# Four edits to a vision tower on one core: order of clearing, maxima and weight loads; routing constants placed once; the wait for sent rows moved

## The reference

```
h = tok(x)                                   # linear projection of patches
h = LN(h + mlstm(h));      h = LN(h + bit_ffn(h))
h = LN(h + performer(h));  h = LN(h + attention_and_moe_gelu(h))   # 8 experts, top 2
h = LN(h + spectral(h));   h = LN(h + moe_swiglu(h))               # 16 experts, top 2, + 2 shared experts
h = LN(h + quantised_attention(h)); h = LN(h + moe_relu(h))        # 8 experts, top 1
```

## Time and profile before

| what | value |
| --- | --- |
| runs of the kernel | 2841.95, 2848.2, 2851.45 us; median 2848.2 |
| profiled execution: own time | 2844.44 us |
| its span, first to last instruction | 2842.6 us |
| busy PE / DVE / ACT / POOL | 2283.0 / 1468.1 / 895.3 / 893.9 us |
| mean granted PE clock | 0.853 of full |
| moved by transfers | 225.44 MB, mean 79 GB/s |
| stages, from about: route gelu, blocks | 956, 1034 us |
| spectral, route swiglu, shared | 1250, 1662, 1713 us |
| blocks swiglu, quantised, route relu, blocks | 1966, 2325, 2620, 2667 us |

### The profile page before, as it was taken

The page is one execution under the profiler, slowest core; times in us unless marked ns, Lnnn a source line. Parts: engine busy times, 40 slices in busy tenths (PEclk is TensorE's granted clock), DMA queues, the critical chain, the costliest instruction groups (busy, mean ns, idle before and its releaser), DMA issues. The chain is left out here.

```text
span 2842.6 us, 47911 instructions
## 1 busy us (share of the span) xinstructions
PE 2283.0 (80%) x18049; PEld 2006.4 (71%) x18049; DVE 1468.1 (52%) x3564; ACT 895.3 (31%) x1923; POOL 893.9 (31%) x809
## 2 busy tenths in 40 slices
PE   7999975599699759956888967998999977553793
PEld 7888863477588649954666667998999966532692
DVE  2667766456577632237888852222442236846313
ACT  0333326423154213324454411111111113754112
POOL 0332325600110342245665406000111136443424
PEclk9989975599799769977999968999999988555696
DMA  9500000060000435530000006001666631000453
GB/s 258 169 1 1 1 1 18 12 201 2 1 2 2 142 103 173 176 95 15 10 10 5 1 2 244 1 1 75 214 213 213 208 124 41 1 1 2 168 176 90
DMA packets 127066, 225.44 MB, mean 79 GB/s; under 512 B 17201, under 2 KB 97645, under 8 KB 119798
## 3 DMA queue, kind: packets, MB, share of 16 engines
q1 hardware_dynamic: 116278, 204.09, 21.9%
q0 software_dynamic: 10560, 18.29, 2.2%
...
## 5 line engine op out<-in xcount | busy, mean ns | idle before, releaser
L2513 POOL COPY bl_swiglu_w<-ahead_w2swiglu_w 128x1152 f32 x53 | 60.7, 1148 | 478.0 <-PE psum L2557 275.4
L2539 PE MATMUL psum<-bl_swiglu_xt,bl_swiglu_w 128*128 128x128 f32 x1272 | 153.0, 277 | 4.6 <-DMA bl_swiglu_w<-in_swiglu_w 3.6
L2539 PEld LDWEIGHTS psum<-bl_swiglu_xt,bl_swiglu_w 128*128 128x128 f32 x1272 | 151.0, 194 | 5.2 <-DMA bl_swiglu_w<-in_swiglu_w 4.0
L2581 ACT ACTIVATE bl_swiglu_sg<-psum 128x384 f32<-128x384 f32 x106 | 52.0, 490 | 310.5 <-PE psum L2546 310.5
L2608 DVE COPY bl_swiglu_xt<-psum 128x256 f32<-128x256 f32 x53 | 22.5, 424 | 206.5 <-PE psum L2524 206.5
L2692 PE MATMUL psum<-tower_xT,shared_w 128*128 128x216 f32 x528 | 103.1, 353 | 18.9 <-DMA shared_w<-in_shared_w 18.9
L2593 ACT ACTIVATE bl_gelu_hid<-psum,bl_gelu_w 128x128 f32<-128x128 f32 x270 | 74.5, 375 | 124.4 <-PE psum L2546 124.4
L2692 PEld LDWEIGHTS psum<-tower_xT,shared_w 128*128 128x128 f32 x528 | 98.5, 195 | 19.7 <-DMA shared_w<-in_shared_w 19.1
L2557 PE MATMUL psum<-bl_swiglu_w,bl_swiglu_hid 128*128 128x192 f32 x636 | 112.1, 326 | 0.0
L2737 DVE TENSOR_TENSOR shared_hid<-shared_sg,psum 128x432 f32<-128x432 f32 x66 | 39.9, 604 | 134.1 <-ACT shared_sg L2728 128.6
L2513 POOL COPY bl_gelu_w<-ahead_w2gelu_w 128x1350 f32 x45 | 58.9, 1312 | 152.5 <-DVE bl_gelu_y L2628 137.2
...
## 6 DMA issues: line engine op xcount, KB each, us to landing
...
```

What stands on the lines that cost most here:

```text
L2513: pool.tensor_copy(w2[:, n % DEEP], w2all[:, e, :].rearrange("p e n -> p (e n)")).then_inc(s_w2, 1)
L2539: pe.matmul(up_tile(n, j, i, side), w[:, o:o + 128], xt[:, n % 2, side, :], start=(i == 0), stop=False, skip_group_check=True)
L2581: act.activation(sg[:, j], bank_pair(n, j)[:, 0, 0:3 * BLOCK].rearrange("p (i n) -> p i n", i=3), ACT.Silu).then_inc(s_silu, 1)
```

## The change

1. A new ahead plan's transfers go before older ones in `coming`.
2. The routing constants (14 transfers: eight constants, two parts of each of three gate weights) get SBUF for the whole run and are loaded once, by SP in the performer stage before it clears the shelves. The routings wait on the one semaphore `laid`. The seed column is copied by DVE into `base`. The table `blocks` becomes a row `count` that is broadcast. Each routing has two semaphores less, the blocks one less and no gb transfer.
3. The shared experts' weights become an ahead plan. `load_ahead` now also runs in swiglu's route, with the four shared weights, swiglu's second weights (9216 KB) and the quantised stage's; the shared stage's PE waits on one semaphore that SP raises when all of these have landed.
4. POOL no longer waits for its sent rows in the routings; SP waits for them in the blocks stage, between the first block's weights and its rows. For the first three blocks weights are issued ahead of rows; later blocks keep rows ahead of weights. POOL's own wait in the shared stage stays.
5. Spectral: only the edges of hs that must be zero and its row of ones are cleared, ahead of power(0); fetch(1), fetch(2) and the clearing of zz come after it; power(2) moves ahead of the wait for theta and angles(0).
6. Quantised: POOL's clearing of sel and q3 moves behind its power and fetch loop; the maxima of q, k and v are taken one pair later than that of h; the casts into sel move into the score loop.

The diff, cut to its core:

```diff
@@ -137,7 +137,7 @@
         for key, plan in self.plans:
             self.key = key
             self.cst["ahead"][key], dmas = plan(self, self.A)
-            self.cst["coming"] += dmas
+            self.cst["coming"] = dmas + self.cst["coming"]
         return self
...
@@ -1387,6 +1387,7 @@
             def _(sp):
                 S.arrived(sp, s_w)
                 S.clear_before(sp)
+                lay_constants(sp, cst)
                 clear_rows(sp, cst, 1)

...
+def routing_constants(S, cst, A):
+
+    new = {"iota": ([T, 16], A["iota"][:, 0]), "earlier": ([T, T], A["before"]), "ones": ([T, T], A["ones"][0:T, 0:T]),
+           "seed": ([T, 16], A["seed"]), "count": ([1, MAXB], A["blocks"]), "upto": ([16, 3, 16], A["upto"]),
+           "steps": ([16, 1], A["steps"]), "gb": ([128, 4], A["gelu_gb"])}
+    cst["laid"], cst["lay"] = S.sem("laid"), []
+    for name, (shape, src) in new.items():
+        cst[name] = S.sb(name, shape)
+        cst["lay"].append((cst[name][:], src))
+    for kind, E in EXPERTS.items():
+        w = cst["wg" + kind] = S.sb("wg" + kind, [128, 2, E])
+        cst["lay"] += [(w[:, 0], A[kind + "_gate"][0:128]), (w[64:128, 1], A[kind + "_gate"][128:D])]
+
+
+def lay_constants(sp, cst):
+
+    for dst, src in cst["lay"]:
+        sp.dma_start(dst, src).then_inc(cst["laid"], 16)
+
...
 def make_route(kind):
...
-            wg = S.sb("wg", [128, 2, E])
-            iota = S.sb("iota", [T, 16])
-            before = S.sb("before", [T, T])
-            ones = S.sb("ones", [T, T])
-            blocks = S.sb("blocks", [1, MAXB, E])
-            upto = S.sb("upto", [16, 3, 16])
-            steps = S.sb("steps", [16, 1])
-            gb = S.sb("gb", [128, 4])
+            wg, iota, before, ones, count, upto, steps, gb = [
+                cst[k] for k in ("wg" + kind, "iota", "earlier", "ones", "count", "upto", "steps", "gb")]
+            laid, all_laid = cst["laid"], 16 * len(cst["lay"])
...
-            (s_w, s_late, s_z, p_T, c_T, p_l, c_lo, c_m, p_m, c_slot, v, c_all, p_n, c_nb, p_e, c_d, c_e) = S.sems(
-                *"w late z p_T c_T p_l c_lo c_m p_m c_slot v c_all p_n c_nb p_e c_d c_e".split())
-            early = [(wg[:, 0], A[kind + "_gate"][0:128]), (wg[64:128, 1], A[kind + "_gate"][128:D]),
-                     (iota[:], A["iota"][:, 0]), (base[:, 0], A["seed"][:, 0:E]), (before[:], A["before"]),
-                     (ones[:], A["ones"][0:T, 0:T])] + ([(gb[:], A["gelu_gb"])] if gelu else [])
-            late = [(blocks[:], A["blocks"][:, :, 0:E]), (upto[:], A["upto"]), (steps[:], A["steps"])]
+            (s_z, p_T, c_T, p_l, c_lo, c_m, p_m, c_slot, v, c_all, p_n, c_nb, p_e, c_d, c_e) = S.sems(
+                *"z p_T c_T p_l c_lo c_m p_m c_slot v c_all p_n c_nb p_e c_d c_e".split())

...
-                    for dst, src in early:
-                        sp.dma_start(dst, src).then_inc(s_w, 16)
-                    for dst, src in late:
-                        sp.dma_start(dst, src).then_inc(s_late, 16)
                     S.clear_before(sp)
-                    if kind != "swiglu":
-                        S.load_ahead(sp)
+                    S.load_ahead(sp)
...
                 def _(pool):
...
-                        pool.wait_ge(cst["sent"], cst["sent_count"])
...
-                    pe.wait_ge(s_w, 16 * len(early))
+                    pe.wait_ge(laid, all_laid)
                     done = 0
...
                     if gelu:
                         for p in range(3):
                             level(p)
-                    dve.wait_ge(s_w, 16 * len(early))
+                    dve.wait_ge(laid, all_laid)
+                    K.then(dve.tensor_copy(base[:, 0], cst["seed"][:, 0:E]))
...
@@ -2260,7 +2268,7 @@
                         dve.tensor_tensor(lo[:, :, 0:E], lo[:, :, 0:E], highest, ALU.subtract).then_inc(c_d, 1)
                     dve.wait_ge(p_e, 1)
                     upper = lambda j: bank(UP)[:, j * E:(j + 1) * E]
-                    K.then(dve.tensor_tensor(past[:, 0], blocks[:, 0:NB], upper(1)[0:1].unsqueeze(1).broadcast_to([1, NB, E]), ALU.is_ge))
+                    K.then(dve.tensor_tensor(past[:, 0], count[:, 0:NB].unsqueeze(2).broadcast_to([1, NB, E]), upper(1)[0:1].unsqueeze(1).broadcast_to([1, NB, E]), ALU.is_ge))
...
@@ -2452,14 +2460,14 @@
             hid = S.sb("hid", [128, 2, KC, BLOCK])
             sg = S.sb("sg", [128, 2, 3, BLOCK])
             y = S.sb("y", [128, 2, D])
-            gb = S.sb("gb", [128, 4])
+            gb = cst["gb"]
...
             with nc.Block() as block:
                 @block.sync
                 def _(sp):
-                    def fetch_block(n):
+                    def fetch_rows(n):
                         if n >= DEEP:
                             sp.wait_ge(p_T, n - DEEP + 1)
                         b = bass.ds(sp.value_load(place[0:1, n:n + 1], min_val=0, max_val=E * DEPTH - 1), 1)
                         sp.dma_start(xr[:, n % DEEP], shelves[b].rearrange("b p n -> (b p) n")).then_inc(s_x[n % DEEP], 16)
+
+                    def fetch_weights(n):
                         e = bass.ds(sp.value_load(owner[0:1, n:n + 1], min_val=0, max_val=E - 1), 1)
                         if n >= DEEP:
...
                     S.clear_before(sp)
-                    if kind == "gelu":
-                        sp.dma_start(gb[:], A["gelu_gb"]).then_inc(s_gb, 16)
                     for n in range(DEEP):
-                        fetch_block(n)
+                        fetch_weights(n)
+                        if n == 0:
+                            sp.wait_ge(cst["sent"], cst["sent_count"])
+                        fetch_rows(n)
                     S.arrived(sp, s_all)
                     for n in range(NB):
                         if n + DEEP < NB:
-                            fetch_block(n + DEEP)
+                            fetch_rows(n + DEEP)
+                            fetch_weights(n + DEEP)
...
+
+def weights_shared(S, A):
+
+    w1 = [S.sb(f"w1{x}", [128, 3 * 768]) for x in range(SHARED)]
+    w2 = [S.sb(f"w2{x}", [128, 6, D]) for x in range(SHARED)]
+    return (w1, w2), [pair for x in range(SHARED) for pair in (
+        (w1[x][:], A["shared_w1"][x]), (w2[x][:].rearrange("p k n -> p (k n)"), A["shared_w2"][x]))]
...
-        w1 = [S.sb(f"w1{x}", [128, 3 * HID]) for x in range(N)]
-        w2 = [S.sb(f"w2{x}", [128, KC, D]) for x in range(N)]
+        w1, w2 = cst["ahead"]["shared"]
         hid = S.sb("hid", [128, 2, KC, C])
         sg = S.sb("sg", [128, 3, 2, C])
...
-        s_up, s_silu, s_hid, s_dn, s_acc = S.sems("up", "silu", "hid", "dn", "acc")
+        s_w, s_up, s_silu, s_hid, s_dn, s_acc = S.sems("w", "up", "silu", "hid", "dn", "acc")
...
         with nc.Block() as block:
             @block.sync
             def _(sp):
+                S.arrived(sp, s_w)
                 S.clear_before(sp)
-                for x in range(N):
-                    sp.dma_start(w1[x][:], A["shared_w1"][x]).then_inc(s_w[x], 16)
-                    sp.dma_start(w2[x][:].rearrange("p k n -> p (k n)"), A["shared_w2"][x]).then_inc(s_w[x], 16)
-                S.load_ahead(sp)
...
-                    pe.wait_ge(s_w[x], 32)
+                    pe.wait_ge(s_w, 1)
...
                             pe.wait_ge(s_hid, (n - 1) * 3 + j + 1)
@@ -2899,18 +2915,22 @@
                         C_.fetch(pool, 2 * p + 1)

                 fetch(0)
+                for b in range(2):
+                    hi = hs[0:CH, b].rearrange("p s k (g n) -> p s k g n", n=IMG)
+                    for s in range(1, 4):
+                        ins = pool.memset(hi[:, s, :, :, 0:s], 0.0)
+                F_.then(ins)
+                F_.then(pool.memset(hs[CH:CH + 1, :, 0, 1, :], 1.0))
+                C_.power(pool, 0)
                 fetch(1)
-                F_.then(pool.memset(hs[0:CH], 0.0))
-                F_.then(pool.memset(hs[CH:CH + 1], 1.0))
-                C_.power(pool, 0)
-                fetch(2)
                 F_.then(pool.memset(zz[:], 0.0))
                 shifts(0)
+                fetch(2)
                 C_.power(pool, 1)
                 fetch(3)
+                C_.power(pool, 2)
                 pool.wait_ge(s_theta, 1)
                 angles(0)
-                C_.power(pool, 2)
                 fetch(4)
                 scales(0)
                 shifts(1)
@@ -3394,13 +3414,13 @@
                 pool.memset(rnd[:, 1:2], -ROUND).then_inc(s_fix, 1)
                 for t in range(WAY):
                     C_.fetch(pool, t)
-                pool.memset(sel[:], 0.0).then_inc(s_fix, 1)
-                pool.memset(q3[:], 0.0).then_inc(s_fix, 1)
                 for p in range(NP):
                     C_.power(pool, p)
                     if p + 2 < NP:
                         C_.fetch(pool, 2 * p + 4)
                         C_.fetch(pool, 2 * p + 5)
+                pool.memset(q3[:], 0.0).then_inc(s_fix, 1)
+                pool.memset(sel[:], 0.0).then_inc(s_fix, 1)
...
@@ -3732,6 +3752,8 @@
```

(21 more changed lines are left out.)

18 lines of the change are left out of this document (8 added, 10 removed).

## The result

The changed kernel takes 2808.17 us (median of four runs, 2806.78 to 2818.38) where the kernel before takes 2848.53 (2841.95 to 2851.45): ratio 0.9869, 95% interval 0.984 to 0.9898, 37 us by the ratio and 40 by the medians.

What follows compares the result with a forecast made beforehand. Stages bounded by their last engine at each barrier, with standing at the edges. Terms −4.8 − 7.3 − 2.4 − 8.9 + 0.3 − 7.2 − 4.0 = −34.3 us, from the 2848.2 median 2813.9, given as 2814; range 2803 to 2828.

Steps and rivals of the forecast that it cites:

- first stage: First stage, where transfers set the end: the new order of ahead loads was to stay within ±1 us.
- shared: Shared stage: with weights loaded ahead, TensorE starts 0.2 after the barrier; −8.9 us, bounds −9.2 and 0.
- quantised: Quantised stage: clears moved from the start, maxima out of the loop's circle, casts costing some; −7.2 us (0 to −10).
- spectral: Spectral stage: fewer clears bring keys 8.3 us earlier, running sums 7.3; −7.3 us, bounds −3 and −8.3.
- Constants and waits: Routings: constants in place bring logits 2.9, 2.4 and 2.5 us earlier; the moved sent wait gives 1.5 in gelu and relu.
- gelu term: Gelu routing and blocks: constants 2.9, sent wait 1.5, fewer clears and transfers 0.4; −4.8 us (−3.3 to −6.5).
- late-weights rival: Shared stage: weights come late under one semaphore for 13.6 MB, costing up to 8.9 us (2823); chance 0.10.
- TensorE's circle: Quantised loop: TensorE's work for a pair put at 6.2 to 6.8 us, a possible limit after the maxima move.
- The casts: Quantised score loop: casts into sel cost 0.6 alone, up to 3.6 behind GpSimd's roundings; +1.3 us taken.
- Power(2)'s new wait: Spectral stage: GpSimd waits for VectorE's third pair ahead of the angles; the lead falls from 8.3 to 7.3 us, bound −3.
- Blocks: Expert blocks' opening, weights before rows: 0 in gelu (bounds −1.1 and +1.3), +0.3 us in swiglu, ±0 in relu.
- slower rival: Shared stage: TensorE's clock might stay low after the earlier start; +150 us (2964) if half stays low; chance 0.04.

Runs made afterwards that it cites:

- e3: Changed kernel with GpSimd's wait for sent rows back at the end of the gelu and relu routings, none on SyncE; ratio to the kernel before 0.9906.
- e6: Changed kernel with the ahead loads issued at the shared stage's opening instead of in swiglu's routing, still under one semaphore; ratio to the kernel before 1.002.
- e8: The kernel before, unaltered, profiled a second time; ratio 0.9998.
- e7: Changed kernel with sel cleared and cast by VectorE ahead of its first keys in the quantised stage; ratio to the kernel before 0.9869.
- e1: The changed kernel, unaltered, run again; ratio to the kernel before 0.990.
- e5: Changed kernel with the quantised maxima of q, k and v taken in the same turn as that of h again; ratio to the kernel before 0.9905.
- e2: Changed kernel with a new plan's ahead loads put behind the older ones again; ratio to the kernel before 0.9884.
- e9: Changed kernel with each of the first three blocks' rows issued ahead of its weights, SyncE's sent wait before both; ratio to the kernel before 0.9882.
- e10: Changed kernel with the new order of ahead loads undone, a second draw of that kernel; ratio to the kernel before 0.9885.
- e11: The changed kernel, unaltered, run once more on another chip; ratio to the kernel before 0.9889.
- e4: Changed kernel with the spectral stage's third power behind the first angles again; ratio to the kernel before 0.9869.

## Why the forecast held, step by step

The forecast was 2814, a gain of 34; 37 by the ratio came. The mechanism of each term was there, but that the total is so close is partly luck. The first stage, shared and quantised brought 8.4 more than was put, spectral, the gelu and the relu blocks 7.4 less, and these nearly cancel.

**Constants and waits** (rows 1, 3, 4, 8 and 16): sized right. 2.7, 2.4 and 2.5 at the three openings against 2.9, 2.4 and 2.5; 1.7 and 1.1 for the moved wait against 1.5 each (e3). The drain was held to go with the number of sends and to start at once. That fits gelu, where it ends 3.6 after the last send; in relu it ends 2.4 after, 0.6 more than the 1.85 of the earlier trace rows. The range of the gelu term, −3.3 to −6.5, does not follow from its parts, which give −2.0 to −6.1; routing and blocks together brought −2.5, outside the one and inside the other.

**Shared**: the step was right, and its margin too: 299 GB/s needed, 414 had; landed 39 after the routing's opening, where 38 to 46 was put. 8.9 became 10.3 since the clock also rose 2.9 after the first matmul in place of 6.0. The late-weights rival was put at a cost of up to 8.9. That is too little: e6 has TensorE wait 44 where before had it wait 9, so the whole queue late makes the stage 34 longer than in the kernel before. In the changed kernel the loads land 10 us ahead of the barrier.

**Quantised**: the circle was right and the choice inside its bounds was the cautious one. The working does not add up as written: 4.1 at the start and ten turns at 0.44 are the 8.5 that was taken, and with the maxima's 1.6 off, as the text says, it is 6.9, with bounds of 4.5 and 10.5 in place of 12.4. What came is 12.3 at the last power (72.4 for 84.7), as GpSimd's 6.2 a pair was the limit from the first turn on. At the first rounding behind the loop 10.7 was left, which is the 1.6. The stage is 10.1 shorter than in the first profile of before; the 11.3 of the table has 1.2 of e8's longer loop in it. TensorE's circle, for whose sake 0.44 of the possible 0.8 a turn was taken, never showed.

The casts were put at 1.3 and took 1.12. Three casts took 3.15 beside GpSimd's one long clear, 1.12 beside its roundings, and 0.59 in e7 beside the start of its fetches. The Trainium skill (SBUF — State Buffer, Who interferes with whom) has a cast in its two-port mode and GpSimd block each other for a whole instruction. That is in the first of these numbers. The 3.6 that the prediction worked out from it is the worst case, each cast behind a whole rounding, and the trace of the score loop shows a third of that.

**Spectral**: here the step from the first running sum to the stage's end was mis-sized. The sum had put the lead at 7.3 at the running sums and carried it to the end. It was 6.2 there (power(2) came 41.6 after the opening and not 40.7, and the fetches and scales behind it 0.2 later), and only 2.8 of it were left at the eleventh pair in after, 7.1 in e1. The clock took it. Windows from the third pair's running sum to the fourth's, before and after:

```profile
1374.30:1406.40 32.10, 28.34 (x129) 21.37 (x128) 26.51 (x44) 15.47 (x25) 21.12 (x18) 0.95 0.04 12
```
```profile
1369.30:1402.90 33.60, 29.84 (x128) 22.25 (x128) 26.51 (x44) 15.47 (x25) 21.11 (x18) 0.90 0.04 10
```

The other engines are busy for as long as before, TensorE for 1.5 us longer over the same matmuls, at a granted clock of 0.90 in place of 0.95, and the way is 1.5 us longer. Over the whole way from the first running sum to the barrier the profiles fall into two groups. Both of before take 348.0 and 348.1 us, with 30.5 and 30.6 us of them at the lower clock level; e1, e3, e5 and e6 take 347.4 to 348.0, with 30.1 to 30.5. After, e2, e7, e9, e10 and e11 take 351.1 to 352.8, with 40.6 to 42.3. So where the clock is as in before the whole lead reaches the end (stage 404.4 to 406.1), and in six of ten profiles the clock takes 3 to 5 us again. Why it falls more often in some executions of the changed kernel stays open. Power(2)'s new wait, the reason for discounting, is worth nothing at the first running sum either way (e4).

**Blocks**: put at 0 for the reordering; e9 shows +0.4 to +0.7 an edge, inside the stated −1.1 to +1.3. Missed was the clock at these edges. Both profiles of before had it rise 4.2 to 4.4 (gelu) and 3.0 to 3.3 (relu) after the first expert matmul; the changed kernel and its variants have 2.9 to 12.2. One block late costs 1.3 us in twelve matmuls, as in the rows above. Late rises go with long stages: relu's blocks took 132.2 to 132.7 with a rise 8.9 or more after the first matmul and 129.8 to 130.8 with one up to 4.5. The slower rival named the clock, but in the shared stage and at +43 or more; here it is some 2 us at an edge.

**First stage**: costed at ±1, came out 2.9 shorter in these profiles, 2.1 over all of them, with overlap.

## What to carry to other kernels

Read a forecast's price from the stage's edge: four of the gains here (three openings of routings, the start of the shared stage) were one row of idle time in front of a first instruction, and each came back within 0.2 us. Before one semaphore is made to stand for a queue of loads, work out at what rate the last of them lands in time, since missing it costs the whole queue (44 us) and not one tensor. In a loop of several engines, take the work that waits for the newest result out of the circle; here the pitch then fell from 7.1 to 6.2, GpSimd's own work for a pair (e5 against after).

## What the chip showed beyond that

**The clock's rise moves from one execution to the next.** Behind the same matmuls it came 2.9 to 12.2 us after the first of them. Of the 22 edges of gelu's and relu's blocks in the eleven profiles of the changed kernel and its variants, six came after 8.9 us or more, the others within 5.2. The four edges of the kernel before came at 3.0 to 4.4; two profiles are too few to say whether the change makes the late ones likelier. A single profile can be wrong by 2 us in an edge's stage and by 8 in mlstm (363.3 to 371.9, with 73 to 89 us at the lower level). Stages whose time at the lower level repeats (performer 37 us, attention 18) repeat to 0.3.

**Two other chips, 49 us slower for the kernel before.** Windows at the shared stage's start, after on the first chip and e11 on the third (same kernel):

```profile
1709.00:1759.00 50.00, 50.00 (x325) 47.19 (x326) 10.93 (x21) 9.17 (x16) 37.72 (x39) 0.97 0.21 63
```
```profile
1705.00:1755.00 50.00, 25.94 (x111) 18.68 (x112) 4.62 (x13) 3.40 (x5) 35.59 (x36) 0.67 0.20 59
```

While GpSimd sends, TensorE is busy for 25.9 of 50 us there in place of 50.0, at a granted clock of 0.67 in place of 0.97, and the timeline has it standing with no releaser but its own instructions' issue; after the sends it runs on at full rate. The stage takes 287.7 against 241.5. The two routings in which GpSimd sends are longer as well, gelu's 78.0 against 73.2 and relu's 45.0 against 43.3; the swiglu routing, without sends, takes 48.5 on every chip. These three stages make 53 us, and the changed kernel's times are 55 to 59 longer there (2863.5 and 2867.1 against 2808.2). The kernel before loses 48 to 50, so the change brings 31 to 33 us on these chips where it brought 37 to 40 on the first; the intervals of the ratios overlap. The stages of the kernel before were not profiled there. What makes these chips slower was not tried.
